# Dealing three mix products over the last filter steps, and tying the loads of record groups 2 to 5 to earlier gathers, in a graph layer with attention and experts

## The reference, cut to what matters

```python
xn = _layernorm(x)
# graph part, per edge: a filter of the edge times the row of its neighbour, summed by node
h = shifted_softplus(f_ij @ Wf1 + bf1)
W = (h @ Wf2 + bf2) * rcut_ij[:, None]
...                                   # messages x_ij from W, xs[idx_j], xv[idx_j] and the directions
agg = jax.ops.segment_sum(x_ij, idx_i, num_segments=n)
...
# mix part
q = softmax(q, axis=-1); k = softmax(k, axis=-1)
context = einsum('bhnd,bhne->bhde', k, v)
out = einsum('bhnd,bhde->bhne', q, context)
mix = out.transpose(0, 2, 1, 3).reshape(b, n, h * d) @ Wo + bo
x = x + gnn + mix
x = x + experts(_layernorm(x))        # two of eight experts per node
```

## Time and profile before

| | |
|---|---|
| median of 3 runs | 1278.21 us (1277.85 to 1278.65) |
| the profiled execution's own time | 1278.83 us |
| its span, first instruction to last | 1276.8 us |
| PE busy | 1187.3 us (93%) |
| DVE, ACT, POOL busy | 1066.9, 812.8, 873.4 us |

### The profile page before, as it was taken

How to read it: one execution, slowest core, us unless ns; L and a number is a source line. 1 busy time by engine, 2 the same in 40 slices (tenths; PEclk the granted TensorE clock), 3 DMA queues, 4 the chain that set the end, 5 groups by cost and what they waited for, 6 DMA issues and landing times.

```text
span 1276.8 us, 16203 instructions
## 1 busy us (share of the span) xinstructions
PE 1187.3 (93%) x4096; PEld 699.3 (55%) x4096; DVE 1066.9 (84%) x1973; ACT 812.8 (64%) x1822; POOL 873.4 (68%) x795
## 2 busy tenths in 40 slices
PE   4999999989998999799999999999999999976995
PEld 3666666767766664244444444444444444865882
DVE  5959999899888995789999999999999896678335
ACT  3677777767777660667667677677677674873330
POOL 6357777777777775688888888888888780053650
PEclk8989999999999999999999999999999999967996
DMA  9248876888899966988888888889889871544557
GB/s 274 67 157 296 299 280 247 307 304 290 293 312 327 309 238 252 344 297 312 313 301 315 312 304 312 312 298 315 297 314 311 298 245 59 181 166 139 183 168 231
DMA packets 106607, 337.65 MB, mean 264 GB/s; under 512 B 16782, under 2 KB 17802, under 8 KB 100372
## 3 DMA queue, kind: packets, MB, share of 16 engines
q0 software_dynamic: 57264, 188.75, 41.2%
q1 hardware_dynamic: 49252, 147.88, 35.2%
HBM read 211.27 MB, written 125.30 MB: 264 GB/s over the span
## 4 chain that ended last, share of the span: by engine, by line
PE 71%; DVE 11%; DMA 9%; issue 4%; POOL 2%; ACT 2%; SPq 1%; DVEq 0%; POOLq 0%; ACTq 0%
PE PS L2300 20%; PE PS L2305 20%; PE PS L2236 9%; PE PS L2427 6%; DVE RR L1586 4%; DMA edge_records<-RR 3%; PE PS L2106 2%; PE PS L2116 2%; PE PS L2084 2%; DMA RR<-node_table,RR 2%; DMA X<-in_x 2%; POOL edge_records L953 1%; DVE h_low L1579 1%; POOL expert_inputs L1020 1%; PE PS L2407 1%
## 5 line engine op out<-in xcount | busy, mean ns | idle before, releaser
L990 POOL DMA_INDIRECT RR<-node_table,RR x322 | 443.5, 1377 | 115.1 <-issue 66.5
L1250 ACT ACTIVATE RR<-RR 128x256 f32<-128x256 f32 x966 | 394.5, 495 | 195.0 <-PE PS L2305 151.9
L953 POOL DMA_INDIRECT edge_records<-RR x316 | 317.2, 1004 | 104.8 <-issue 72.9
L2300 PE MATMUL PS<-RR 128*125 128x512 f32 x644 | 290.0, 593 | 6.2 <-DVE RR L1763 6.2
L2305 PE MATMUL PS<-RR 128*125 128x512 f32 x644 | 289.6, 592 | 0.0
L2300 PEld LDWEIGHTS PS<-RR 128*125 128x125 f32 x644 | 120.2, 188 | 163.7 <-issue 148.9
L2305 PEld LDWEIGHTS PS<-RR 128*125 128x125 f32 x644 | 120.8, 188 | 155.5 <-issue 155.5
L1586 DVE TENSOR_TENSOR RR<-PS,RR 128x512 f32<-128x512 f32 x237 | 160.5, 685 | 19.8 <-PE PS L2236 19.0
L2236 PE MATMUL PS<-wf_high,h_high 128*128 128x512 f32 x316 | 148.2, 469 | 12.9 <-DVE RR L1586 12.7
L1763 DVE TENSOR_TENSOR RR<-RR 128x1536 f32<-128x1536 f32 (+1 forms) x81 | 140.9, 1740 | 0.0
L2236 PE MATMUL PS<-wf_low,h_high 128*128 128x512 f32 x316 | 125.2, 396 | 0.0
(11 more groups left out here) (350 smaller groups left out, 1795.5 us busy)
## 6 DMA issues: line engine op xcount, KB each, us to landing
RR<-edge_records SPq DMA_DIRECT2D x48, 1040.0 KB, 6.8
expert_inputs<-RR SPq DMA_DIRECT2D x8, 2313.0 KB
RR<-edge_records SPq DMA_DIRECT2D x27, 520.0 KB, 5.3
RR<-edge_records SPq DMA_DIRECT2D x15, 780.0 KB, 5.5
RR<-in_L_ffn_beta_w SPq DMA_DIRECT2D x8, 1024.0 KB
expert_w_raw<-in_L_ffn_expert_w SPq DMA_DIRECT2D x8, 1024.0 KB, 7.2
RR<-edge_records SPq DMA_DIRECT2D x31, 260.0 KB, 5.0
edge_records<-RR POOLq DMA_INDIRECT x322, 4.1
```

Source lines behind the costliest of these rows:

```text
L953: g.indirect_dma_start(out=rec_dram, out_offset=place, in_=ST[:, j, :], in_offset=None).then_inc(scattered[c], 16)
L990: g.indirect_dma_start(out=GB[q % GBS][:, t, 1:5, :].rearrange("p k n -> p (k n)"), out_offset=None, in_=tab_dram, in_offset=bass.Indirect ...
L1250: last = a.activation(message_slot(q)[:, t, k:k + 5:4, :], GB[q % GBS][:, t, 0:k + 3:k + 2, :], ACT.Copy, scale=record_slot(q)[:, t, 4 * C ...
L2300: te.matmul(PS[0:NT, 2 * (r % PSS), :], OH[q % OHS][:, t, 0:NT], GB[q % GBS][:, t, 1:5, :].rearrange("p k n -> p (k n)"), start=(n == 0), ...
```

## The change

Two edits that touch the same stretch.

The mix products of node tiles 0, 1 and 2, twelve matmuls, are taken out of the loop behind the filter steps and dealt, one at a time, to the ends of steps 68 to 77 (place `j` = 3), and two to step 78 (places 1 and 3). All three use PSUM bank 6. `add_mix(0)` and `add_mix(1)` move into DVE's steps 72 and 76, `add_mix(2)` behind its last step. In the loop that is left (tiles 3 to 9) DVE no longer has `scalar_parts(0)`, `scalar_parts(1)` and `messages(0)` between the additions: they stand behind all ten.

For groups 2 to 5 SP, before it issues the load, now waits until all gathers of the group two before have landed.

```diff
+        DEALT = 3
+        deal_at = [(WO_STEP + KD + u, 3) for u in range(DEALT * KD - 2)] + [(STEPS - 1, 1), (STEPS - 1, 3)]
+        dealt_in = [deal_at[n * KD + KD - 1][0] for n in range(DEALT)]
+        def mix_bank(n):
+            return 6 if n < DEALT else 6 + n % 2
...
                 if q == LATE_RECORDS:
                     sp.wait_ge(y_psum, NB)
+                if 2 <= q < RBS:
+                    sp.wait_ge(gathered[(q - 2) % GBS], gathers(q - 2))
...
                 column(i, c, 1)
+                if m - 1 in dealt_in[:-1]:
+                    add_mix(dealt_in.index(m - 1))
...
+            add_mix(DEALT - 1)
             mixing_weights()
             zero_sums(0)
-            for n in range(NB):
...
+            for n in range(DEALT, NB):
+                done = 2 * (n - DEALT)
+                for part in range(done + 1, min(done + 3, ZERO_PARTS)):
+                    zero_sums(part)
                 add_mix(n)
-                if n == 6:
...
+            for c in range(RING):
+                dve.wait_ge(scattered[c], landed(c))
+            dve.wait_ge(empty_scattered, 16 * (NCOL - LOOPED))
+            dve.wait_ge(acc_zero, ZERO_PARTS)
+            scalar_parts(0)
+            for t in range(TPQ):
+                onehot_of(0, t)
+            scalar_parts(1)
+            messages(0)
+            for t in range(TPQ):
+                onehot_of(1, t)
             scalar_parts(2)
...
+            def mix_product(n, k):
+                last = te.matmul(PS[0:NT, mix_bank(n), :], XTQ[:, n, k, :], MO[:, k, :], start=(k == 0),
+                                 stop=(k == KD - 1))
+                if k == KD - 1:
+                    last.then_inc(y_psum, 1)
+            def dealt_mix(u):
+                n, k = divmod(u, KD)
+                if u == 0:
+                    pe.wait_ge(mo_ready, KD)
+                elif k == 0:
+                    pe.wait_ge(mix_added, n)
+                mix_product(n, k)
...
+                elif (m, j) in deal_at:
+                    dealt_mix(deal_at.index((m, j)))
...
-            for n in range(NB):
+            for n in range(DEALT, NB):
                 mix(n)
```

More of the change, by code:

```diff
@@ L659, in gps_layer @@
         assert BB_STEP < STEPS and WO_STEP + KD < BB_STEP
+        DEALT = 3
+        deal_at = [(WO_STEP + KD + u, 3) for u in range(DEALT * KD - 2)] + [(STEPS - 1, 1), (STEPS - 1, 3)]
+        assert deal_at[-3][0] == STEPS - 2
+        dealt_in = [deal_at[n * KD + KD - 1][0] for n in range(DEALT)]
+        def mix_bank(n):
+            return 6 if n < DEALT else 6 + n % 2
         SHIFT_SLOT, COMB_SLOT = X8, X8 + 4
@@ L1630, in add_mix @@
                 dve.wait_ge(y_psum, n + 1)
-                v.tensor_tensor(X[0:NT, n, :], X[0:NT, n, :], PS[0:NT, 6 + n % 2, :], ALU.add)\
+                v.tensor_tensor(X[0:NT, n, :], X[0:NT, n, :], PS[0:NT, mix_bank(n), :], ALU.add)\
                     .then_inc(mix_added, 1)
@@ L1790, in messages @@
                 message_b(q)
+            add_mix(DEALT - 1)
             mixing_weights()
             zero_sums(0)
-            for n in range(NB):
[L1795 to L1799, removed]
-                add_mix(n)
-                if n == 6:
[L1802 to L1814, removed]
+            for n in range(DEALT, NB):
+                done = 2 * (n - DEALT)
+                for part in range(done + 1, min(done + 3, ZERO_PARTS)):
+                    zero_sums(part)
+                add_mix(n)
+            for c in range(RING):
[9 more added lines that the diff above has]
+                onehot_of(1, t)
             scalar_parts(2)
@@ L2159, in router_gamma @@
                 last.then_inc(gam_psum, 1)
+            def mix_product(n, k):
[10 more added lines that the diff above has]
+                mix_product(n, k)
             def mix(n):
-                if n == 0:
-                    pe.wait_ge(mo_ready, KD)
+                if n == DEALT:
                     pe.wait_ge(router_ready, 1)
-                if n >= 2:
+                else:
                     pe.wait_ge(mix_added, n - 1)
                 for k in range(KD):
-                    last = te.matmul(PS[0:NT, 6 + n % 2, :], XTQ[:, n, k, :], MO[:, k, :], start=(k == 0),
-                                     stop=(k == KD - 1))
-                last.then_inc(y_psum, 1)
+                    mix_product(n, k)
             def beta(e):
```

## The result

The changed kernel took 1284.45 us (median of 5 runs, 1282.58 to 1286.44), the kernel before beside it 1277.85 (5 runs, 1277.54 to 1278.65). The ratio is 1.0050, 95% interval 1.0034 to 1.0065: slower, by about 6.4 us. The profiled execution took 1284.45 us with a span of 1282.4; against the profiled execution of before, 1278.83, that is 5.6 us.

The account below looks back on a forecast made before the run. Bound: the start of `sums(3)` at 542.13, after which PE runs without a gap. Waits land group 4's gathers at 541.3 against 537.16, 4.1 us later: 1278.83 becomes 1282.9, less 0.62 to the median, 1282.3; range 1277.0 to 1287.0.

Parts of the forecast that it names:

- the chain of hops: Gathers of group 0, load of 2, gathers of 2, load of 4, gathers of 4: `sums(3)` 4.1 us later; chance 0.50.
- signs of being wrong: Prediction wrong if group 4's gathers land before 537, or PE shows new gaps behind group 3.
- The sum: Issue and landing times added from group 0's gathers (507.4) to group 4's (541.3, against 537.16): 4.1 us later.
- The clock: PE idling before `sums(1)` and `sums(3)` may halve its clock: up to 1.7 us, making 1284.0; not in the forecast.
- the odd groups: Groups 1, 3, 5: group 5's first gather about 537.6 against 532.35, partly slack, leaving about the same 4 us.
- Flood: Held loads of groups 5 to 8 go out together, slowing group 5's gathers; `sums(4)` at 556, 1285 to 1287; chance 0.12.
- I add nothing for it: Group 5's gathers, 5 us later, were given no delay beyond the 4.1 us of group 4.
- Empty rings: At the start, loads and gathers land nearly as when alone: -2.5 to +2.5 us, 1275.7 to 1280.7; chance 0.25.
- The rule on turns: DMA engines alternate between queues by packet, so gathers speed up without unneeded loads; alone it gives about 1278.2.
- Its gain buys nothing here: The mix ends 4 to 8 us earlier, but group 4's load waits on SP until 524.2 anyway.
- PE's end of the filters: With twelve products dealt into steps 68 to 78, PE finishes the filters 6.3 to 10.3 us later, at 486.7 to 490.7.
- late scatters: Dealt products stall PE over 3.6 us beyond their own time, delaying POOL's scatters: 1284.7; chance 0.04.

Follow-up runs that it names:

- 2: Kernel before plus only the waits on SP, all mix products left behind the filter steps; ratio 1.0058 to before.
- 4: Changed kernel with each wait one group closer, on the gathers of the group just before; 1308.94 us, ratio 1.0252 to before.
- 7: Changed kernel plus 36 unread identity products on PE ahead of `sums(3)`, filling its idle gap; ratio 1.0069 to before.
- 1: Changed kernel without the waits on SP, only the dealt mix products; 1277.14 us, ratio 0.9992 to before.
- 5: Changed kernel plus a wait holding the load of group 6 until group 4's gathers landed; 1288.11 us, ratio 1.0088 to before.
- 10: Changed kernel waiting only for loads of groups 4 and 5, on gathers three groups back, with two tiles dealt, not three; ratio 1.0003 to before.

## Why the prediction was right, point by point

**The verdict and the mechanism.** Slower, by the chain of hops behind the waits on SP; 2 and 4 show that the waits alone do it and that their spacing sets the price. The time, 1284.45, lies in the range, 2.2 us above the 1282.3. One of my own signs of being wrong did show: PE has a gap behind group 3 that was not there before, 0.28 us ahead of `sums(8)`. A second wait, ahead of `sums(4)`, is hidden behind the half clock of `sums(3)`.

**The sum.** Most hops came out near what was worked: group 0's gathers at 506.90 (507.4 in the sum), load of 2 at 507.63 (508.15), 6.09 us (6.1), group 2's gathers at 524.01 (523.45), load of 4 at 524.82 (524.2), 4.85 us (6.1), group 4's first gather at 530.47 (531.15). Two terms were mis-sized. Group 4's last gather, for which I kept the 6.40 of before, took 7.81, near the end of 8.0 that the range had; the load of 4 took 4.85 in place of 6.1. That these nearly cancel is luck. The gathers of group 2 were slower too (4.45 us from the first issue to the last in place of 3.75, and 5.05 to the landing in place of 4.6), and the hops cost 5.2 us in place of 4.1.

**The clock.** The forecast took none of it into the sum and named a price of up to 1.7 us inside. `sums(3)` took 1.77 us more, and 7 shows the cause; but only some 0.5 us of it moved the time, since `sums(4)` would have waited for group 5's gathers until 555.47 all the same. The warning of the Trainium skill, "TensorE: Matmul & The Clock Gate", section "Why this matters for your kernels", is borne out in its direction; the gap here, 2.14 us, is shorter than those that it warns of. That the 1284.0 which it gave is nearer than my number is luck: what filled the place of the clock's price was the odd groups.

**Flood**, held at 0.12, came together with the forecast. Its loads went out behind one another from 532.83, and where it put the landing of group 5's gathers (551) and `sums(4)` (556), DVE waited for them until 550.60 (the last of them took 7.7 us) and `sums(4)` began at 555.95. The step of the prediction that failed is "I add nothing for it": the odd groups did not give "about the same 4" but 6.4 (555.33 and 0.14 to the sums, against 549.07), and would have set the time had the clock stayed high. Group 3's gathers landed near 532.1 (529.9 in the prediction), and group 5's first gather went out at 539.04 (537.6). So hops, clock and flood overlap in the same 6.9 us, and are no sum. That the time is 1284.45 and not flood's 1285 to 1287 is what is given back behind, 1.3 us from `sums(4)` to the end of the span, which I had not counted.

**Empty rings** fell, by two places of five. Group 0's last gather (3.54), group 2's (5.05) and the load of 4 (4.85) lie inside its prices or below them; the load of 2 (6.09) and group 4's last gather (7.81) do not, and the latter decides. Alone, gathers take 3.7 and a load 4.8, as that case had it, but only in 4, where a gate of one group leaves them alone. The rule on turns of the Trainium skill, "DMA: Bandwidth & Descriptors", section "Queues, rings and completion order", fits the rows (8.65 us in 1 against 3.7 in 4), though no run here shows the turns themselves. That it would make up for the waits does not follow.

**The mix.** "Its gain buys nothing here" is right, by 2. Alone it lets the load of 4 go out 10 us earlier, where I had 4 to 8, and buys nothing either, by 1. Mis-sized was PE's end of the filters: 483.9, in place of 486.7 to 490.7. PE filled its 4 us of gaps (46.81 busy of 46.88 us in the stretch of the first row) and ran 3.4 us beyond 480.35, though eleven products at 0.858 are 9.4. A part of the 2 us between is likely in how busy time is counted. Filter passes that follow one another start 0.23 us apart (479.89 and 480.12 in the timeline of before) but are recorded as 0.39 long, so at each of the ten gaps in that stretch the row counts some 0.16 us of idle time as busy: by this estimate 1.6 us more room than the 4.0 that I read. It had no effect, since POOL's last scatter was issued at 493.86 (493.99 in the earlier trace rows), so *late scatters* did not occur.

## What to carry to other kernels

A wait that ties a load to work of n items back is a loop: add up the round trip (release, issue, landing, next stage's issue, its landing) and divide by n. If the result is more than the consumer's time for an item, expect to lose about the difference for each item, less what slack there was: here with n = 2 about 17 us for two groups against PE's 13.7, with n = 1 about 14 for one against 6.9; with n = 3 nothing that the runs can tell. And before holding transfers back to speed up others, look at how busy the DMA engines are: at 0.91, as here, holding left them idle (0.77), and what was held came out in one burst on top of the next group (5).

## What the runs showed of the hardware

An idle gap ahead of a burst could cost the clock, but its length alone did not tell when. A gap of 2.14 us was followed by 0.50 in the changed kernel, one of 2.41 us by 1.00 in the kernel before; busy times by stretch, the gap and the sums behind it:

```profile
522.60:525.01 2.41, 0.00 (x0) 0.03 (x1) 2.41 (x3) 2.41 (x7) 0.00 (x0) 1.00 0.99 399
525.01:528.52 3.51, 3.51 (x8) 1.58 (x9) 1.59 (x6) 1.80 (x5) 1.32 (x2) 1.00 1.03 430
```

Ahead of the 2.14 us PE had idled 9.19 and 3.96 us, ahead of the 2.41 only 1.91 and 0.21 us. But work without a pause before a gap doesn't save the clock either: those 1.91 us stood behind 31.06 us of mix products without a gap, and 0.50 followed; in 10, 2.01 us were followed by 3.67 us for eight matmuls, full clock. What decides was not found.

The landing of the same transfer varied by more than I had expected from its company: a gather took 3.3 us at the least in the changed kernel and 9.3 at the most in the kernel before, a load of 1040 KB 4.76 alone (4) and 13.4 as the last of several (7, issued at 539.24).
